# The last edge attention of a four-layer graph network: fp32 one-hots written by ScalarE from a square and a Relu

## The chip, the cores and the metric

The kernel runs on one core of a Trainium2 chip. The metric is the device time of one launch in microseconds (us). The engines are TensorE (PE, its weight loads are PEld), VectorE (DVE), ScalarE (ACT), GpSimd (POOL) and SyncE (SP, which here only issues DMAs). Each engine runs its own instructions in order, and semaphores tie them together.

## The reference, cut to what matters

Four graph layers follow one another on 3125 nodes with 256 features and 103125 edges that are sorted by destination. The change touches the edge part of the last one:

```
rel    = rel_w[edge_relations]
mod_k  = K[src] + 0.2 * rel[:, None, :]
scores = einsum('ehd,ehd->eh', Q[dst], mod_k) / D ** 0.5
seg_max = segment_max(scores, dst, num_segments=N)
ex     = exp(scores - seg_max[dst])
denom  = segment_sum(ex, dst, num_segments=N)
agg    = segment_sum((ex / denom[dst])[:, :, None] * V[src], dst, num_segments=N)
```

## The kernel before, in words

**Items and blocks.** `attention_items` is used twice: as stage `l0e` (with `first` true) for layer 0 and as stage `l3e` for the last layer. An item is 512 edges (G = 4 groups of 128, one edge per partition) that all go to one block of 128 nodes; there are NI = 228 items. Four items (BI = 4) are handled as one batch m, and there are 57 batches. Below, an item's place in its batch is called position 0, 1, 2 or 3. All loops are written out in full by Python, so each engine's order is the order of the code.

**One-hots.** Three kinds say which node an edge belongs to. `ohT` (bf16, node on the partition; L809) turns queries from nodes to edges on PE. `ohrT` (L812) does it for the 64 relations. `oh` (bf16, edge on the partition; `onehots`, L800) is written by DVE for a whole batch, 128x2048 at once, from the row of 0..127 and each edge's local node number. It is used in two places: PE's `spread` (L993) multiplies it with `flT` to hand each run's maximum to the node, and ACT's `widen` (L1045) copies it for one item at a time to fp32 as `ohf`, which PE's `sums` (L1011) multiplies with the weighted values `vw`.

**DVE, at step t** (item n = t+4): for position 1 the batch's `candidates` (L845, L847, waits for `spread`) and `block_max`; `rescale` (L888); `keys` of item n (L819: relation added to the key; waits for the gather and for PE's queries), `products` (L824), `merge` (L895), `scores` (L829); after position 2 `turned_onehots(m+2)` (L809, L812); after position 3 `onehots(m+1)` (L800); then its part of `weigh` (L879, L880) for item t-1.

**PE, at step t:** for position 0 `turn_scores` (L977); `queries(n+1)` (L963, L970); for position 0 `turn_ends` (L983, L984) and `spread` (L991 and 16 matmuls of L993); `sums(t-2)` (L1011).

**ACT, at step t** (y = t-1): for position 1 `weights` (two Exp: L1068, L1072); `widen(y)`; 4 of the 12 multiplications of `weigh(y)` (L1054); for position 0 `turned_ends` (L1062), which writes `flT` for `spread`; then the other 8 multiplications.

**POOL** gathers the keys and values: four indirect DMAs per item (L777), into a ring of SK = 10 items; the gather of item n waits until ACT and DVE have weighed item n-10.

**SP** is one queue. At the first item of each batch it issues `load_rows`: `drow` (L724), then `erow` (L728), and the latter waits for DVE's `ohrT` of the batch before:

```
if m >= 1:
    sp.wait_ge(ohrT_ready, m)
sp.dma_start(erow[:, :], ...)
```

Behind it in the same queue stand the loads of the queries `qb` (L736) and the stores of finished items (L742, for which `merge` waits four items later).

## Time and profile before

| | us |
|---|---|
| median of 3 runs | 6733.41 (6720.29 to 6738.31) |
| profiled execution | 6684.46 |
| its span, first to last instruction | 6682.8 |

| engine | busy us in the span | share |
|---|---|---|
| PE | 4332.2 | 65% |
| DVE | 3454.5 | 52% |
| ACT | 2182.9 | 33% |
| POOL | 3176.4 | 48% |

The stages follow one another and have different limits. `l3e` fills about the last quarter, from 4925 to 6545 us once it runs. A busy share over the whole span says little about it; the rows below are of this stage unless they say otherwise. In a timeline a line is: start us, duration us, engine, source line, operation, output<-input, shapes, count merged, and in brackets how long the engine had been idle before and what released it.

### The profile page before, as it was taken

How to read it: one execution, taken by the hardware profiler on the slowest of the kernel's cores; microseconds unless marked ns; L12 is line 12 of the kernel's file. 1: busy time of each engine (PE TensorE's matmuls, PEld its weight loads, DVE VectorE, ACT ScalarE, POOL GpSimd, SP SyncE). 2: the span in 40 equal slices, each digit the busy share in tenths (PEclk: the TensorE clock that was granted, in tenths of full speed). 3: DMA queues.
4: the chain of work that ended last, by engine and by line, in shares of the span. 5: the costliest groups of instructions: out<-in, count | busy, mean ns of one | idle time of the engine just before them, and what ended most of it. 6: DMA issues, size and time to landing. Idle time of an engine off the chain costs nothing. (4 is left out here: it accounts for less than half of the span.)

```text
span 6682.8 us, 90484 instructions
## 1 busy us (share of the span) xinstructions
PE 4332.2 (65%) x24913; PEld 3133.4 (47%) x24913; DVE 3454.5 (52%) x6689; ACT 2182.9 (33%) x7656; POOL 3176.4 (48%) x3187
## 2 busy tenths in 40 slices
PE   6996667777777734545444537887646666666666
PEld 4664445554444423333333436775335555555553
DVE  4453666666666661212211231112558888888885
ACT  1222455555555430000000111222224554445551
POOL 0422566666666137667766520002155565665551
PEclk8897777777777876767676778998878888888885
DMA  4334666666666525333333407872366666666673
GB/s 134 126 124 163 187 199 201 200 199 199 201 199 197 115 79 185 93 93 92 91 93 93 69 34 254 269 252 86 110 197 203 199 208 203 204 207 196 204 188 102
DMA packets 509934, 1077.05 MB, mean 161 GB/s; under 512 B 94770, under 2 KB 322388, under 8 KB 505993
## 3 DMA queue, kind: packets, MB, share of 16 engines
q0 software_dynamic: 204144, 617.42, 32.6%
q1 hardware_dynamic: 296854, 452.03, 20.2%
q10 hardware_dynamic: 8512, 2.74, 0.2%
q8 instruction: 168, 2.75, 0.2%
q14 instruction: 256, 2.10, 0.1%
HBM read 964.49 MB, written 194.54 MB: 173 GB/s over the span
## 5 line engine op out<-in xcount | busy, mean ns | idle before, releaser
L777 POOL DMA_INDIRECT l3e_kv<-t_table,k_recs x912 | 969.6, 1063 | 677.8 <-ACT l3e_vw L1054 376.5
L777 POOL DMA_INDIRECT l0e_kv<-t_table,k_recs x912 | 969.1, 1063 | 636.7 <-ACT l0e_vw L1054 374.8
L1469 PE MATMUL l2e_pA<-l2e_row,l2e_oh 128*128 128x257 f32 x1824 | 623.6, 509 | 780.2 <-issue 315.1
L1423 POOL DMA_INDIRECT l2e_row<-t_table,l2e_idx x912 | 900.7, 988 | 388.0 <-issue 268.0
L1469 PEld LDWEIGHTS l2e_pA<-l2e_row,l2e_oh 128*128 128x128 f32 x1824 | 454.0, 258 | 949.5 <-issue 862.0
L1011 PE MATMUL l0e_pA<-l0e_vw,l0e_ohf 128*128 128x260 f32 x1824 | 650.8, 492 | 199.0 <-issue 138.8
L963 PE MATMUL l3e_pQE<-l3e_qb,l3e_ohT 128*128 128x256 bf16 x2736 | 424.6, 316 | 412.1 <-issue 386.1
L1054 ACT ACTIVATE l0e_vw<-l0e_kv,l0e_w 128x64 f32<-128x64 f32 x2736 | 679.9, 334 | 0.0
L1054 ACT ACTIVATE l3e_vw<-l3e_kv,l3e_w 128x64 f32<-128x64 f32 x2736 | 679.7, 334 | 0.0
L1448 DVE SCALAR_TENSOR_TENSOR l2e_acc<-l2e_acc,k_itf,l2e_pA 128x257 f32<-128x257 f32 x228 | 109.9, 482 | 1059.8 <-issue 978.3
L1011 PEld LDWEIGHTS l0e_pA<-l0e_vw,l0e_ohf 128*128 128x128 f32 x1824 | 412.7, 239 | 366.6 <-issue 219.8
L1011 PE MATMUL l3e_pA<-l3e_vw,l3e_ohf 128*128 128x260 f32 x1824 | 532.9, 442 | 7.7 <-ACT l3e_vw L1054 7.2
L963 PEld LDWEIGHTS l3e_pQE<-l3e_qb,l3e_ohT 128*128 128x128 bf16 x2736 | 296.2, 111 | 513.5 <-issue 434.7
L963 PE MATMUL l0e_pQE<-l0e_qb,l0e_ohT 128*128 128x256 bf16 x2736 | 449.7, 326 | 72.7 <-issue 55.9
L1480 ACT ACTIVATE moe_agg<-l2e_acc 128x257 f32 x228 | 95.3, 418 | 1217.1 <-DVE l2e_acc L1448 613.5
L1011 PEld LDWEIGHTS l3e_pA<-l3e_vw,l3e_ohf 128*128 128x128 f32 x1824 | 373.7, 216 | 77.5 <-ACT l3e_vw L1054 9.8
L963 PEld LDWEIGHTS l0e_pQE<-l0e_qb,l0e_ohT 128*128 128x128 bf16 x2736 | 312.5, 116 | 190.5 <-issue 93.3
L819 DVE TENSOR_TENSOR l3e_kv<-l3e_kv,l3e_pD 128x1024 f32<-128x1024 f32 x228 | 276.0, 1211 | 171.5 <-DMA t_agg<-l0e_acc 92.5
L1971 POOL DMA_INDIRECT comb_ya<-t_yslot,k_slot x52 | 51.9, 999 | 602.8 <-POOLq L68 582.2
L1045 ACT ACTIVATE l3e_ohf<-l3e_oh 128x512 f32<-128x512 bf16 x228 | 141.0, 619 | 499.7 <-PE l3e_pA L1011 374.3
L824 DVE TENSOR_TENSOR l0e_prod<-l0e_pQE,l0e_kv 128x1024 f32<-128x1024 f32 x228 | 276.3, 1212 | 33.8 <-DMA t_table<-l0n_tab 33.3
L824 DVE TENSOR_TENSOR l3e_prod<-l3e_pQE,l3e_kv 128x1024 f32<-128x1024 f32 x228 | 279.2, 1224 | 7.8
(469 smaller groups left out, 7118.9 us busy)
## 6 DMA issues: line engine op xcount, KB each, us to landing
exp_w<-in_L_gnn_w SPq DMA_DIRECT2D x224, 512.0 KB
t_table<-l0n_tab SPq DMA_DIRECT2D x26, 2048.0 KB, 6.9
l0e_qb<-t_q SPq DMA_DIRECT2D x228, 192.0 KB
l3e_qb<-t_q SPq DMA_DIRECT2D x228, 192.0 KB
t_agg<-l0e_acc SPq DMA_DIRECT2D x228, 130.0 KB
t_agg<-l3e_acc SPq DMA_DIRECT2D x228, 130.0 KB
l0e_drow<-t_drow SPq DMA_DIRECT2D x57, 512.0 KB
l3e_drow<-t_drow SPq DMA_DIRECT2D x57, 512.0 KB
```

What stands on the lines that cost most here:

```text
L777: pool.indirect_dma_start(kv[:, n % SK, g, :], None, table[:, :], bass.IndirectOffsetOnAxis(ap=K["recs"][:, n, g, ridx:ridx + 1], axis=0)) ...
L819: dve.tensor_tensor(key, key, pR.unsqueeze(2).to_broadcast([P, G, H, DK]), ALU.add).then_inc(key_done, 1)
L824: dve.tensor_tensor(prod[:, n % 2, :, :], pQE[n % 2][:, :, :], kv[:, n % SK, :, 0:D], ALU.mult).then_inc(prod_done, 1)
L963: last = pe.matmul(pQE[n % 2][:, g, :], ohT[:, m % 2, G * j + g, :], qb[:, n % QL, i, :], start=(i == 0), stop=(i == 2))
L1011: last = pe.matmul(pA[n % 2][:, 0:H * HV], ohf[:, n % 2, g, :], vw[:, v, g, :, :].rearrange("p h c -> p (h c)"), start=(g == 0), stop=(g = ...
L1045: act.activation(ohf[:, n % 2, :, :], oh[:, m % 2, G * j:G * j + G, :], ACT.Copy).then_inc(ohf_ready, 1)
L1054: last = act.activation(vw[:, v, g, h, 0:DK], kv[:, n % SK, g, D + h * DK:D + (h + 1) * DK], ACT.Copy, scale=w[:, m % 2, j, g, h:h + 1])
L1423: pool.indirect_dma_start(row[:, s, g, 0:D], None, table[:, :], bass.IndirectOffsetOnAxis(ap=idx[:, i, g:g + 1], axis=0)).then_inc(row_rea ...
L1448: dve.scalar_tensor_tensor(out=acc[:, s, :], in0=acc[:, before, :], scalar=K["itf"][:, i, 1:2], in1=pA[s % 2][:, 0:W], op0=ALU.mult, op1=A ...
L1469: last = pe.matmul(pA[s % 2][:, 0:W], oh[:, s, g, :], row[:, s, g, :], start=(g == 0), stop=(g == G - 1))
L1480: last = act.activation(all_agg[:, bass.ds(b, 1), :].rearrange("p b c -> p (b c)"), acc[:, s, :], ACT.Copy)
L1971: pool.indirect_dma_start(ya[:, t % U, k, :], None, T["yslot"][:, :], bass.IndirectOffsetOnAxis(ap=K["slot"][:, t, k:k + 1], axis=0)).then ...
```

## The change

In the stage of the last layer (`first` false) only:

- DVE no longer writes `oh`, and that tile is gone.
- ACT makes the fp32 one-hot of an item itself, three items ahead: `near(n)` is four Square instructions of 128x128 (local node number minus 0..127, squared), and `at(n)` is one Relu of 128x512 over one minus that. It replaces `widen`.
- `ohf` has six slots instead of two.
- `spread` on PE reads `ohf` in fp32 instead of `oh` in bf16, so `flT`, `crow` and `oneb` become fp32 too. It now waits until all four items of the batch are ready.
- `run` is laid over a constant tile to save room.

```diff
+        OS = 2 if first else 6
-        oh = S.sb("oh", [P, 2, BI * G, P], BF16)
+        oh = S.sb("oh", [P, 2, BI * G, P], BF16) if first else None
+        FT = BF16 if first else F32
+        flT = S.sb("flT", [P, BI * G, 2, H], FT)
+        crow = S.sb("crow", [1, BI * G, 2, H], FT)
+        oneb = S.sb("oneb", [1, P], FT)
+        ohf = S.sb("ohf", [P, OS, G, P])
...
-                if j == 3 and m + 1 < NBT:
+                if first and j == 3 and m + 1 < NBT:
                     onehots(m + 1)
...
             def spread(m):
-                pe.wait_ge(oh_ready, m + 1)
+                if first:
+                    pe.wait_ge(oh_ready, m + 1)
+                else:
+                    pe.wait_ge(ohf_ready, BI * (m + 1))
...
+                    spot = oh[:, m % 2, c, :] if first else ohf[:, (BI * m + c // G) % OS, c % G, :]
...
+            def near(n):
+                if n >= OS:
+                    act.wait_ge(a_ps, n - OS + 1)
+                for g in range(G):
+                    last = act.activation(ohf[:, n % OS, g, :], K["iota"][:, :], ACT.Square, bias=K["dlf"][:, n, g:g + 1], scale=-1.0)
+                last.then_inc(near_done, 1)
+
+            def at(n):
+                act.wait_ge(near_done, n + 1)
+                act.activation(ohf[:, n % OS, :, :], ohf[:, n % OS, :, :], ACT.Relu, bias=K["ones"][:, 0:1], scale=-1.0).then_inc(ohf_ready, 1)
...
             for t in range(0, NI + 1):
                 m, j = divmod(t, BI)
                 y = t - 1
                 if live(m) and j == 1:
                     weights(m)
+                if not first and t + 3 < NI:
+                    near(t + 3)
                 if y >= 0:
-                    widen(y)
+                    if first:
+                        widen(y)
                     weigh(y, 0, 1)
+                if not first and t + 3 < NI:
+                    at(t + 3)
                 if live(m) and j == 0:
                     turned_ends(m)
```

## Rows read from the trace of the kernel before

**Rows 1.** Busy time per engine of the running stage (stage windows; us, busy us, count).
```profile
4925.00:6545.00 1620.00, 1092.71 (x9187) 832.53 (x9184) 1332.59 (x2314) 814.87 (x3135) 931.03 (x872) 0.82 0.67 197
```
**Rows 2.** What DVE waited for, 5100 to 6500: total us, times, longest.
```profile
DVE l3e_kv L819 <- PE l3e_pD L970: 51.0, 33, 3.4
DVE l3e_kv L819 <- DMA t_agg<-l0e_acc: 47.1, 38, 5.5
DVE l3e_cand L845 <- PE l3e_pC L993: 46.6, 40, 2.8
```
**Rows 3.** What SP's queue waited for in the same stretch.
```profile
SPq L728 <- DVE l3e_ohrT L812: 457.5, 29, 19.2
```
**Rows 4.** Timeline of one batch, from DVE's turned one-hots to the keys of position 0.
```profile
5711.34 0.74 DVE L812 TENSOR_SCALAR l3e_ohrT<-l3e_erow,k_pidx 64x2048 bf16<-64x2048 bf16 x1
5712.11 0.48 SPq L728 DMA_DIRECT2D l3e_erow<-t_erow  x1
5713.70 0.00 SPq L736 DMA_DIRECT2D l3e_qb<-t_q  x1
5716.83 2.28 DVE L800 TENSOR_TENSOR l3e_oh<-k_iotab,k_dlb 128x2048 bf16<-128x2048 bf16 x1
5717.69 2.72 PE L963 MATMUL l3e_pQE<-l3e_qb,l3e_ohT 128*128 128x256 bf16 x12 [6.89 <-issue]
5720.35 0.81 PE L970 MATMUL l3e_pD<-l3e_relw,l3e_ohrT 64*128 64x64 bf16 x12
5721.27 1.22 DVE L819 TENSOR_TENSOR l3e_kv<-l3e_kv,l3e_pD 128x1024 f32<-128x1024 f32 x1 [1.41 <-issue]
```
**Rows 5.** Timeline: keys of position 0 (first and last batch) and one held merge.
```profile
4944.67 1.22 DVE L819 TENSOR_TENSOR l3e_kv<-l3e_kv,l3e_pD 128x1024 f32<-128x1024 f32 x1 [1.79 <-PE l3e_pD L970]
5027.81 0.43 DVE L895 TENSOR_TENSOR l3e_acc<-l3e_part,l3e_pA 128x260 f32<-128x260 f32 x1 [4.95 <-DMA t_agg<-l3e_acc]
6471.09 1.22 DVE L819 TENSOR_TENSOR l3e_kv<-l3e_kv,l3e_pD 128x1024 f32<-128x1024 f32 x1 [2.45 <-PE l3e_pD L970]
```
**Rows 6.** Timeline of the same batch: from sums to candidates.
```profile
5721.09 2.02 PE L1011 MATMUL l3e_pA<-l3e_vw,l3e_ohf 128*128 128x260 f32 x8
5723.06 1.47 PE L963 MATMUL l3e_pQE<-l3e_qb,l3e_ohT 128*128 128x256 bf16 x12
5723.21 0.63 ACT L1045 ACTIVATE l3e_ohf<-l3e_oh 128x512 f32<-128x512 bf16 x1 [8.73 <-PE l3e_pA L1011]
5726.17 0.28 ACT L1062 ACTIVATE l3e_flT<-l3e_pC 128x128 bf16<-128x128 bf16 x1 [1.38 <-PE l3e_pC L984]
5726.60 0.21 PE L991 MATMUL l3e_pC<-l3e_crow,l3e_oneb 1*128 1x128 bf16 x1 [1.55 <-ACT l3e_flT L1062]
5726.74 0.56 PE L993 MATMUL l3e_pC<-l3e_flT,l3e_oh 128*128 128x8 bf16 x16
5727.33 0.22 DVE L845 COPY l3e_cand<-l3e_pC 128x64 f32<-128x64 f32 x1 [1.08 <-PE l3e_pC L993]
```
**Rows 7.** Timeline, fp32 passes that keep PE full: 64 and 128 moving columns.
```profile
3843.16 0.56 PE L1748 MATMUL gate_wide<-moe_wg,gate_xT 128*128 128x64 f32 x4
4302.74 2.05 PE L1863 MATMUL exp_pH<-exp_xT,exp_w 128*128 128x128 f32 x16
```
**Rows 8.** Timeline, the batch before: a gather released by ACT, and keys of position 2.
```profile
5700.94 0.94 POOL L777 DMA_INDIRECT l3e_kv<-t_table,k_recs  x1 [3.62 <-ACT l3e_vw L1054]
5706.83 1.22 DVE L819 TENSOR_TENSOR l3e_kv<-l3e_kv,l3e_pD 128x1024 f32<-128x1024 f32 x1 [1.02 <-DMA t_agg<-l0e_acc]
5707.97 0.95 POOL L777 DMA_INDIRECT l3e_kv<-t_table,k_recs  x1 [2.33 <-ACT l3e_vw L1054]
5708.13 2.96 ACT L1054 ACTIVATE l3e_vw<-l3e_kv,l3e_w 128x64 f32<-128x64 f32 x12
```
**Rows 9.** Groups by line: ACT with 256 and with 512 columns.
```profile
L2232 ACT ACTIVATE l3n_kv<-l3n_pK 128x512 f32<-128x512 f32 x12 | 7.1, 591 | 0.0
L2231 ACT ACTIVATE l3n_q<-l3n_pQ 128x256 bf16<-128x256 f32 x12 | 4.6, 384 | 27.3 <-PE l3n_pK L2198 27.3
```
**Rows 10.** Groups by line: the table load after the one Square of the kernel (combine stage).
```profile
L2047 ACT ACT_TABLE_LOAD x1 | 1.3, 1283 | 0.0
```

More of the change, by code:

```diff
@@ L654, in attention_items @@
         sc = S.sb("sc", [P, 2, BI * G * H])
-        run = S.sb("run", [BI * G * H, P])
+        run = S.sb("run", [BI * G * H, P]) if first else K["upper"][0:BI * G * H, :]
         fl = S.sb("fl", [BI * G * H, P], BF16)
-        flT = S.sb("flT", [P, BI * G, 2, H], BF16)
-        crow = S.sb("crow", [1, BI * G, 2, H], BF16)
-        oneb = S.sb("oneb", [1, P], BF16)
+        FT = BF16 if first else F32
+        flT = S.sb("flT", [P, BI * G, 2, H], FT)
+        crow = S.sb("crow", [1, BI * G, 2, H], FT)
+        oneb = S.sb("oneb", [1, P], FT)
         cand = S.sb("cand", [P, BI, G, H])
@@ L666, in attention_items @@
         w = S.sb("w", [P, 2, BI, G, H])
-        ohf = S.sb("ohf", [P, 2, G, P])
+        ohf = S.sb("ohf", [P, OS, G, P])
         vw = S.sb("vw", [P, VS, G, H, HV])
@@ L687, in attention_items @@
         vwa_ready, vwd_ready, a_ps, part_done, item_done = (S.sem(k) for k in ("vwa_ready", "vwd_ready", "a_ps", "part_done", "item_done"))
-        key_done, ohrT_ready = S.sem("key_done"), S.sem("ohrT_ready")
+        key_done, ohrT_ready, near_done = S.sem("key_done"), S.sem("ohrT_ready"), S.sem("near_done")
         if first:
@@ L992, in spread @@
                 for c in range(BI * G):
-                    last = pe.matmul(pM[:, c // G, c % G, :, :].rearrange("p k h -> p (k h)"), oh[:, m % 2, c, :], flT[:, c, :, :].rearrange("p k h -> p (k h)"), start=False, stop=(c == BI * G - 1))
+                    spot = oh[:, m % 2, c, :] if first else ohf[:, (BI * m + c // G) % OS, c % G, :]
+                    last = pe.matmul(pM[:, c // G, c % G, :, :].rearrange("p k h -> p (k h)"), spot, flT[:, c, :, :].rearrange("p k h -> p (k h)"), start=False, stop=(c == BI * G - 1))
                 last.then_inc(m_ps, 1)
@@ L1010, in sums @@
                 for g in range(G):
-                    last = pe.matmul(pA[n % 2][:, 0:H * HV], ohf[:, n % 2, g, :], vw[:, v, g, :, :].rearrange("p h c -> p (h c)"), start=(g == 0), stop=(g == G - 1))
+                    last = pe.matmul(pA[n % 2][:, 0:H * HV], ohf[:, n % OS, g, :], vw[:, v, g, :, :].rearrange("p h c -> p (h c)"), start=(g == 0), stop=(g == G - 1))
                 last.then_inc(a_ps, 1)
@@ L1072, in weights @@
                 act.activation(w[:, m % 2, :, :, :].rearrange("p i g h -> p (i g h)"), z[:, :], ACT.Exp).then_inc(w_ready, 1)
+            if not first:
+                for n in range(3):
+                    near(n)
+                    at(n)
             for t in range(0, NI + 1):
```

## The prediction

> **What bounds the kernel now.** I read the stage windows first, then the waits of DVE, then the timeline of one batch on all queues. In the running stage no engine is full: of 1620 us DVE is busy 1333, PE 1093, POOL 931, ACT 815 [rows 1]. So the batch of four items, which takes 1620/57 = 28.4 us, is set by a loop of waits with DVE in it, and the question is whether the instruction that goes (L800) lies on that loop.
>
> The timeline shows the loop. DVE ends the turned one-hots `ohrT` at 5712.08. SP has stood waiting for exactly that, 457.5 us in 29 waits over 1400 us [rows 3], and issues `erow` at 5712.11, and behind it in its queue the query load of position 0 at 5713.70. PE has nothing to do until that load lands, 6.89 us idle, and starts the queries at 5717.69. They take 2.72 us, and 0.81 us for the relations follow. DVE's keys of position 0 start at 5721.27, after an idle of 1.41 us [rows 4]. From the end of `ohrT` to these keys it is 9.2 us, and DVE's own work between them, L800 included, does not fill this. It is not one batch: in the timeline from 4944.67 to 6471.09, 49 of 56 batches have idle time before the keys of position 0, mean over all 1.64 us [rows 5]. The waits of keys for PE and a DMA in 1400 us are 51.0 and 47.1 us [rows 2]; they also hold position 2, below.
>
> The rest of the loop is keys of position 0, `scores`, PE's `spread`, `candidates`, items 1 and 2, and the next `ohrT`: 28.4 - 9.2 = 19.2 us. In it DVE waits for `spread` in 40 of the 49 batches of that stretch, 46.6 us [rows 2].
>
> **The change part by part.**
>
> *L800 goes from DVE.* It takes 2.28 us, 2.2 us of queue time, 57 times, 125 us of DVE's work. It lies after the scores of position 3, between `ohrT` and the keys of position 0 [rows 4]. In 49 of 56 batches the idle before these keys grows by what is removed, and nothing is gained: late next is what was late already, PE waiting for the query load. In the 7 others DVE had been held in `merge` by a store (4.95 us in the batch at 5027.81 [rows 5]) and comes late; these gain at most 2.2 us each. Per batch 2.2 x 7/56 = -0.3 us, bounds 0 and -2.2.
>
> *`spread` in fp32.* No row has an fp32 matmul with 8 moving columns. Now 16 bf16 matmuls take 0.56 us and one more 0.14 us ahead of them: 0.73 us from 5726.60 to `candidates` at 5727.33 [rows 6]. An fp32 matmul shows as two passes, each with its own weight load. The nearest row is 4 passes of 64 columns in 0.56 us, last one 0.22 us long, so one every (0.56-0.22)/3 = 0.113 us [rows 7]. Seventeen matmuls are 34 passes: 34 x 0.113 = 3.84 us, that is +3.1 us. Bounds: if 8 columns cost what the columns cost, a pass is an eighth of 0.113, and with the bf16 spacing of 0.035 us as floor (0.56/16) 34 passes take 1.2 us, +0.5; at twice the spacing 34 x 0.226 = 7.7 us, +7. I take +3.1, because weights of 128 columns are loaded in the nearest row and here alike.
>
> The same 128 columns of weights arrive at 0.035 us in bf16 [rows 6] and at 0.113 us in fp32 [rows 7]. The Trainium skill ("TensorE: Matmul & The Clock Gate", Weight-path perf modes) says why this speaks against the change: a fast weight load exists for 128 weights of any type but fp32, and a load takes columns/1.2 ns, 107 ns. By its figure the 34 passes would be an estimated 3.6 us instead of 3.84.
>
> *ACT.* `widen`, 0.63 us [rows 6], becomes four Squares and a Relu. A 64-column ACTIVATE with a scale from a tile comes every (2.96-0.33)/11 = 0.24 us [rows 8]; 64 columns more cost 64 x (591-384)/256 = 0.05 us [rows 9]. So four Squares take about 1.2 us; the Relu takes 0.6 us like `widen`, since its wait for `near` is covered by four multiplications (1 us). That is +1.2 us per item (bounds +1.0 and +1.6), 270 us of ACT's time: 815 becomes some 1090 of 1620 us, no bound by share. Queued behind it on ACT: (a) `flT` at position 0. ACT starts on the end of `sums` at 5723.21, and `flT` at 5726.17 after 1.38 us idle [rows 6]. New: 5723.21 + 1.2 + 1.0 + 0.6 + 0.1 = 5726.1, just in time. By the same sum over 52 batches the mean delay is 0.33 us (29 have none, 7 have 1.38): +0.3 us. (b) The multiplications of positions 1 to 3, one after another: they end 1.2, 2.4 and 3.6 us later plus what `candidates` is late. PE's `sums` for them come after the query wait, ACT's idle of 8.73 us [rows 6] takes this up. (c) POOL, which waits for ACT with 2.33 and 3.62 us of idle per batch [rows 8]; twelve gathers of 1.25 us fit between, with 2 us to spare.
>
> *What takes up the delay.* Keys of position 2 wait now: 1.02 us at 5706.83, 5.9 us behind the gather at 5700.94 that ACT released [rows 8], and this distance holds for 47 batches. I can't name the mechanism, but that gather follows `flT` and not `spread`, so the idle, 37 us over 56 batches, absorbs -0.7 us of the spread's +3.1. The longer `spread` also moves `sums`, `shift` and `queries` of position 2 by 3.1 us; they were 1.7 us and more ahead. The new wait of `spread` for four one-hots costs nothing: the last is written before `flT` on the same queue. The startup one-hots lie in ACT's idle time. A different table would cost 1.28 us per load [rows 10]; that load stands after the Square there, and none before it, so I put nothing.
>
> *Sum.* Per batch -0.3 + 3.1 + 0.3 - 0.7 = +2.4 to 2.5 us; times 56 = +139 us. In the profiled execution's terms 6684.5 + 139 = 6823. The runs' median lies 49 us above that execution, so the forecast for the median is 6733 + 139 = **6872 us**, and the batch grows from 28.4 to 30.9 us.
>
> **The rivals.**
> *POOL becomes late (slower still).* ACT releases the first gather after `weights` 1.2 + 3.1 us later, the loop moves by 2.5. If keys of position 0 need those gathers, each batch gets another 1 us, and where nothing is absorbed 0.7 more: 6872 + 57 to 97 = 6930 to 6970. For it: 38 keys waits lay to a DMA's account [rows 2]. Against: POOL itself still waits for ACT.
> *PE stays fast.* After 6.89 us idle the queries ran 2.72 us [rows 4] against 1.47 us at 5723.06 [rows 6]. If a late `sums` shortens that gap enough, 1.25 us and 0.3 us of the relations come back: 56 x 1.5 = 87 us, 6785.
> *Passes overlap.* With +0.5 instead of +3.1 for `spread`, all of it is absorbed at position 2 and ACT's +0.3 stays against L800's -0.3: 6733, the same.
> *DVE is the bound (faster).* Decided at the keys of position 0: if the queries land at least 2.2 us before DVE arrives, L800 is worth its full 2.2 us. That needs the query load to come 2.2 us sooner than now, for example because fewer gathers compete with it as ACT releases them late. Then -2.2 + 3.1 + 0.3 - 0.7 = +0.5, and with cheap passes -2.2 - 0.2 = -2.4 us a batch, 6733 - 134 = 6600.
> *The change doesn't do what it says*: Square sits in another table than Exp. Two loads a batch, 2 x 1.28 us on ACT, one of them ahead of `weights`: up to 57 x 2.6 = 146 us on top, 7020.
>
> **How the numbers follow.** Forecast 0.50 (its own range 6830 to 6910); PE fast or partly cheap passes, 6760 to 6830, 0.19; POOL late 0.17; the table 0.03; the same 0.05; faster 0.06. Within 0.3% (20 us) is about what a measurement can tell from no change. Range 6765 to 6965. Faster 0.06, same 0.06, slower 0.88.
>
> **What would show it.** L993 with twice as many records, one every 0.11 us and `candidates` idle before it grown from 1.2 to above 3 us; idle before keys of position 0 near 3.5 us; keys of position 2 hardly idle; POOL still waiting for ACT; PE still 2.72 us in the first queries. I am wrong if the fp32 passes come every 0.05 us or less, if the idle before the keys of position 0 does not grow, or if SP no longer waits for `ohrT`.

## The result, and the profile after

The kernel after takes **7303.18 us** (median of 4 runs, 7299.61 to 7306.93) against 6730.88 (4 runs, 6720.29 to 6738.31): ratio **1.0852**, 95% interval 1.0833 to 1.0870. The forecast was 6872 with a range to 6965. The direction was right, the size was not: +139 us were expected and +572 came, 10.2 us a batch in place of 2.5.

The stage window of the running stage, after (columns as in [rows 1]):

```profile
6000.00:6700.00 700.00, 498.57 (x3256) 405.13 (x3257) 384.39 (x715) 343.91 (x1265) 281.64 (x286) 0.72 0.50 150
```

Against [rows 1] DVE is 55% busy and not 82%, the DMA engines 0.50 and not 0.67, and PE's mean granted clock is 0.72 and not 0.82. Everything got emptier but PE, which is 71% busy and not 67%: a loop of waits has become longer, and PE does its part of it at a lower clock. What DVE, ACT and POOL waited for, 5200 to 6900 (total us, times, longest), answers [rows 2]. DVE waits in two places, ahead of the keys of position 0 and ahead of the candidates:

```profile
DVE l3e_kv L821 <- DMA t_agg<-l0e_acc: 392.7, 39, 10.8
DVE l3e_cand L847 <- PE l3e_pC L999: 299.1, 42, 10.4
```
```profile
ACT l3e_ohf L1057 <- DMA t_table<-l12n_hs: 341.9, 39, 9.1
```
```profile
POOL l3e_kv L779 <- ACT l3e_vw L1071: 820.0, 88, 10.7
```

There are two new waits on DVE: the candidates wait 7.1 us a time for `spread` (299.1/42; before 46.6/40 = 1.2 in [rows 2]), and the keys of position 0 wait 10.1 us a time (392.7/39). The name of a DMA beside the keys is not to be trusted: `t_agg<-l0e_acc` is a transfer of another stage. ACT's Squares (L1057) carry an equally foreign name, and all they wait for in the code is PE's `sums`.

PE's timeline through one `spread` answers [rows 6]:

```profile
5898.94 0.76 PE L996 MATMUL l3e_pC<-l3e_crow,l3e_oneb 1*128 1x128 f32 x2 [0.46 <-ACT l3e_flT L1079]
5899.63 7.00 PE L999 MATMUL l3e_pC<-l3e_flT,l3e_ohf 128*128 128x8 f32 x32
5906.48 3.81 PE L1017 MATMUL l3e_pA<-l3e_vw,l3e_ohf 128*128 128x260 f32 x8
```

The 32 passes take 7.00 us and start every 0.213 us, against 0.113 in [rows 7]. The `sums` behind them take 3.81 us. The same eight passes behind the bf16 `spread` of the kernel before take less:

```profile
5727.15 3.14 PE L1011 MATMUL l3e_pA<-l3e_vw,l3e_ohf 128*128 128x260 f32 x8
```

The stage windows of that stretch after the change (last three columns: granted clock, DMA share, GB/s) say why:

```profile
5898.00:5900.00 2.00, 1.34 (x6) 0.99 (x6) 1.68 (x4) 1.48 (x7) 0.00 (x0) 0.50 0.30 81
5902.00:5904.00 2.00, 2.00 (x11) 2.00 (x11) 0.00 (x0) 0.00 (x0) 1.48 (x2) 0.50 0.83 309
```

PE idles ahead of `spread`, the granted clock has fallen to 0.50 (1.2 GHz) when it begins, and it stays there through 7 us in which PE is busy all the time. So it is in 54 of the 57 batches of this trace.

The batch's other half answers [rows 4]: from DVE's turned one-hots to the keys of position 0, first DVE and PE, then SP and ACT, then POOL's last gather of twelve.

```profile
5917.35 0.74 DVE L814 TENSOR_SCALAR l3e_ohrT<-l3e_erow,k_pidx 64x2048 bf16<-64x2048 bf16 x1
5934.35 1.22 DVE L821 TENSOR_TENSOR l3e_kv<-l3e_kv,l3e_pD 128x1024 f32<-128x1024 f32 x1 [10.69 <-DMA t_agg<-l0e_acc]
```
```profile
5923.57 2.72 PE L965 MATMUL l3e_pQE<-l3e_qb,l3e_ohT 128*128 128x256 bf16 x12 [5.41 <-issue]
5926.23 0.82 PE L972 MATMUL l3e_pD<-l3e_relw,l3e_ohrT 64*128 64x64 bf16 x12
5926.97 2.32 PE L1017 MATMUL l3e_pA<-l3e_vw,l3e_ohf 128*128 128x260 f32 x8
```
```profile
5922.02 0.34 SPq L738 DMA_DIRECT2D l3e_qb<-t_q  x1
5924.15 0.01 SPq L744 DMA_DIRECT2D t_agg<-l3e_acc  x1
5927.73 0.02 SPq L738 DMA_DIRECT2D l3e_qb<-t_q  x1
5932.74 0.71 SPq L744 DMA_DIRECT2D t_agg<-l3e_acc  x1
5934.30 0.34 SPq L738 DMA_DIRECT2D l3e_qb<-t_q  x1
```
```profile
5934.37 1.28 ACT L1057 ACTIVATE l3e_ohf<-k_iota,k_dlf 128x128 f32<-128x128 f32 x4 [9.00 <-DMA t_table<-l12n_hs]
```
```profile
5916.35 1.20 POOL L779 DMA_INDIRECT l3e_kv<-t_table,k_recs  x1 [10.70 <-ACT l3e_vw L1071]
...
5931.22 0.95 POOL L779 DMA_INDIRECT l3e_kv<-t_table,k_recs  x1 [0.30 <-issue]
```

From the end of `ohrT` (5918.09) to the end of PE's relation terms (5927.05) it is 9.0 us, as before: PE was late in the same way. But the keys start only at 5934.35, **7.3 us behind** what they need from PE, and ACT's Squares at 5934.37, 5.1 us behind the end of the `sums` they need (5929.29). Both start again right behind POOL's twelfth gather in a row (ends 5932.17). I call this the late release. Over 56 batches the median distance from PE's relation terms to the keys of position 0 is 6.5 us after and 0.15 us before.

PE's ends are modelled, but the order of PE's work says more. The keys wait for the relation terms and the Squares for the `sums` that run 2.3 us longer on the same engine, and yet both start within 0.02 us of each other, in nine of ten batches. The trace's records of the semaphores agree: the signal of the relation terms is recorded at 5934.26 and that of the `sums` at 5934.35. Had the matmuls themselves run late, the two would lie some 2 us apart, as they do in a trace of this program without the late release, below (1.95 us or more). So the signal of the relation terms was held back when their work was done. Nor is it PE's signals alone. The last semaphore that SP asks for between 5924.15 and 5934.16 was set at 5916.21. But its register instructions, which stand between two DMA issues, come mostly every 0.7 us there, and the issues lie 3.6 and 5.0 us apart. From item 10 to item 218, 367 of 1872 such steps of SP are longer than 0.6 us (325 us in all), and 98 in the kernel before.

### The profile page after: what moved, and what is told of

Same layout as the page of the kernel before. It is cut to its first block and busy times, and to the rows that moved or that the text cites. A ratio compares the mean times of both kernels' runs of the same rounds, so it can differ in the third digit from the quotient of the medians.

```text
span 7299.5 us, 92996 instructions
## 1 busy us (share of the span) xinstructions
PE 4781.4 (66%) x25882; PEld 3576.6 (49%) x25882; DVE 3324.5 (46%) x6632; ACT 2469.2 (34%) x8568; POOL 3090.2 (42%) x3187
## 5 line engine op out<-in xcount | busy, mean ns | idle before, releaser
L779 POOL DMA_INDIRECT l3e_kv<-t_table,k_recs x912 | 902.4, 989 | 1310.1 <-ACT l3e_vw L1071 1053.6
L1071 ACT ACTIVATE l3e_vw<-l3e_kv,l3e_w 128x64 f32<-128x64 f32 x2736 | 695.5, 334 | 0.0
L1017 PE MATMUL l3e_pA<-l3e_vw,l3e_ohf 128*128 128x260 f32 x1824 | 578.3, 471 | 9.8 <-ACT l3e_vw L1071 9.7
L1017 PEld LDWEIGHTS l0e_pA<-l0e_vw,l0e_ohf 128*128 128x128 f32 x1824 | 429.6, 247 | 248.6 <-issue 133.5
L965 PEld LDWEIGHTS l3e_pQE<-l3e_qb,l3e_ohT 128*128 128x128 bf16 x2736 | 299.1, 112 | 443.9 <-issue 362.2
L1017 PEld LDWEIGHTS l3e_pA<-l3e_vw,l3e_ohf 128*128 128x128 f32 x1824 | 405.5, 234 | 89.5 <-ACT l3e_vw L1071 12.5
L1057 ACT ACTIVATE l3e_ohf<-k_iota,k_dlf 128x128 f32<-128x128 f32 x912 | 288.8, 387 | 467.8 <-DMA t_table<-l12n_hs 440.5
L999 PEld LDWEIGHTS l3e_pC<-l3e_flT,l3e_ohf 128*128 128x128 f32 x1824 | 392.3, 331 | 12.5 <-issue 12.1
L999 PE MATMUL l3e_pC<-l3e_flT,l3e_ohf 128*128 128x8 f32 x1824 | 397.7, 361 | 0.0
```

What stands on the lines that cost most here:

```text
L779: pool.indirect_dma_start(kv[:, n % SK, g, :], None, table[:, :], bass.IndirectOffsetOnAxis(ap=K["recs"][:, n, g, ridx:ridx + 1], axis=0)) ...
L965: last = pe.matmul(pQE[n % 2][:, g, :], ohT[:, m % 2, G * j + g, :], qb[:, n % QL, i, :], start=(i == 0), stop=(i == 2))
L999: last = pe.matmul(pM[:, c // G, c % G, :, :].rearrange("p k h -> p (k h)"), spot, flT[:, c, :, :].rearrange("p k h -> p (k h)"), start=Fa ...
L1017: last = pe.matmul(pA[n % 2][:, 0:H * HV], ohf[:, n % OS, g, :], vw[:, v, g, :, :].rearrange("p h c -> p (h c)"), start=(g == 0), stop=(g ...
L1057: last = act.activation(ohf[:, n % OS, g, :], K["iota"][:, :], ACT.Square, bias=K["dlf"][:, n, g:g + 1], scale=-1.0)
L1071: last = act.activation(vw[:, v, g, h, 0:DK], kv[:, n % SK, g, D + h * DK:D + (h + 1) * DK], ACT.Copy, scale=w[:, m % 2, j, g, h:h + 1])
```

## The experiments

Two questions stood at the start: does the fp32 `spread` cost its full length, and does the keys' wait come out of it, or out of ACT's work and POOL's gathers? (The letters A and B in the expectations are theory and rival, as each text works them out.) In each diff lines without a sign are context. All times are beside runs of the kernel before in the same set, whose median is given, because the sets differ by 10%: the kernel before takes 6685 to 6741 us in the first, the second and the fifth ("the slower sets", and the result above was like them), and 6057 us in the third and the fourth ("the faster sets"). The expectations call this a difference of chips. The record doesn't bear that out: it gives the sets the chip numbers 4, 15, 13, 15 and 10, and number 15 has both a slower set (6740.63) and a faster one (6057.48). What makes a set slow is not known.

**First set (before: 6684.79 us).** *17 narrow fp32 matmuls*, whose result nothing reads, ahead of the bf16 `spread`:

```diff
                 pe.wait_ge(flT_ready, m + 1)
+                if not first:
+                    for c in range(17):
+                        pe.matmul(pC[:, 384:392], K["ident"][:, :], K["iota"][:, 0:8], start=True, stop=True)
```

> The kernel before, with 17 fp32 matmuls of 8 moving columns (identity as weights, into unused PSUM columns) in front of the bf16 spread of the last edge attention; ACT and DVE as before. The output is that of before. Theory A (the whole loss is the fp32 spread, and what follows from it): the passes come every 0.22 us, as in the changed kernel, so 34 of them are 7.4 us; candidates wait about 8 us instead of 1.2, and the gathers that ACT releases after candidates start later too, so the keys of position 0 wait as well and the time comes near the changed kernel's: 7200 to 7300 us. Rival B (the fp32 spread is a plain delay, the wait of the keys of position 0 comes from ACT's Squares): +7.4 - 0.7 us a batch, 57 x 6.7 = 380: about 7110, with the idle before the keys of position 0 under 3 us. Rival C (my prediction's price, passes every 0.11 us): 6850 to 6900.

Measured: 7075.64 us, ratio 1.0582 (1.0551 to 1.0613), +391 us or 7.0 a batch. PE's timeline of one batch:

```profile
5727.98 6.51 PE L993 MATMUL l3e_pC<-k_iota,k_ident 128*128 128x8 f32 x34 [1.58 <-ACT l3e_flT L1065]
...
5735.09 3.81 PE L1014 MATMUL l3e_pA<-l3e_vw,l3e_ohf 128*128 128x260 f32 x8
```

The 34 passes alone take 6.7 us in the median (4.3 to 7.4) and the batch pays all of it, in the wait of the candidates (334.1 us in 37 waits from 5100 to 6500). The keys' waits stay near what they were, 41.5 us for PE and 11.0 under a DMA's name, so nothing couples `spread` to them. That is about rival B's size.

*ACT makes the one-hots that `sums` needs*, DVE still writes `oh`, `spread` stays bf16:

```diff
                 if y >= 0:
-                    widen(y)
+                    if first:
+                        widen(y)
+                    else:
+                        near(y)
                     weigh(y, 0, 1)
+                    if not first:
+                        at(y)
```

> The kernel before, with only widen in the last edge attention replaced by four Squares and a Relu for the same item (no lead, two slots); DVE still writes the bf16 one-hots and spread stays bf16. Theory A: ACT's extra 1.2 us per item is nearly hidden, 6730 to 6800 us, candidates still wait 1 to 1.6 us. Rival B: ACT's later release of the gathers is what costs, then this kernel alone shows keys of position 0 waiting 5 us and more and takes 7000 us or more.

Measured: 6833.10 us, 1.0219 (1.0190 to 1.0249), +148 us or 2.6 a batch; the keys wait 123.8 us in 35 waits of the kind with a foreign DMA name. That lies between what the two texts expected. So ACT's work isn't hidden in this set, and 2.6 + 7.0 = 9.6 of the 10.2 us are found in the two parts.

*No gathers past the first ring of ten items:*

```diff
-            for n in range(NI):
+            for n in range(NI if first else SK):
...
-                dve.wait_ge(kv_ready[n % SK], 16 * G * (n // SK + 1))
+                dve.wait_ge(kv_ready[n % SK], 16 * G * (n // SK + 1) if first else 16 * G)
```

The later items compute on stale keys and values.

> The changed kernel; in the last edge attention only the first ring of ten items is gathered and the later items compute on those stale keys and values (part of the work left out, outputs are wrong). Theory A (the keys of position 0 wait until the run of twelve gathers is through): their idle of about 9.3 us goes, the candidates still wait 7 us, and the batch falls from 39.3 to some 31 to 33 us: 6830 to 6950 us. Rival D (the wait belongs to PE or to SP's query loads, not to the gathers): the batch stays above 38 us and the time above 7250.

Measured: 6825.22 us, 1.0208 (1.0178 to 1.0237). The candidates still wait for `spread`, the keys' waits are PE's again (94.9 us in 44 waits), the foreign-named ones are gone: the keys of position 0 start 0.11 us (median) behind PE's relation terms. Of SP's 1872 steps 5 are over 0.6 us. What holds the keys needs POOL's gathers. `spread` is shorter here too, 5.6 us from its start to the candidates (median) where after has 7.7.

*ACT writes bf16 one-hots three items ahead and widens them*; DVE writes none, `spread` is bf16:

```diff
-        FT = BF16 if first else F32
+        FT = BF16
...
-                act.activation(ohf[:, n % OS, :, :], ohf[:, n % OS, :, :], ACT.Relu, ...
+                act.activation(ohb[:, n % OS, :, :], sqf[:, :, :], ACT.Relu, ...
...
-                    if first:
-                        widen(y)
+                    widen(y)
```

> A version of the change that keeps spread in bf16: ACT squares into one fp32 slot, Relu writes a bf16 one-hot three items ahead, and widen copies it to fp32 as before; DVE writes none. ACT does 1.8 us more per item than before. Theory A: with the fp32 spread gone most of the loss is gone, 6720 to 6850 us, candidates wait 1 to 2 us. Rival B (ACT's load is what costs): 7000 us or more, as ACT does more here than in the changed kernel. If DVE's L800 had been on the path, the time would fall to 6650 or below.

Measured: 6950.76 us, 1.0395 (1.0358 to 1.0433). What DVE waited for, 5100 to 6500:

```profile
DVE l3e_kv L823 <- DMA t_agg<-l0e_acc: 418.8, 46, 10.7
...
DVE l3e_cand L849 <- PE l3e_pC L1001: 0.4, 2, 0.2
```

With bf16 the wait for `spread` is gone and the keys' wait is there in full, 9.1 us a time. The two waits have two causes. The time lies between what theory and rival expected: a loss of 4.8 us a batch is left without the fp32 `spread`.

**Second set (before: 6740.63 us): what is it in the gathers?** *Half the bytes*, number and order of the gathers unchanged (the second half of each row stays stale, and half rows are read by whole-row indices, so the results are others):

```diff
-                    pool.indirect_dma_start(kv[:, n % SK, g, :], None, table[:, :],
+                    wid, rows = (2 * D, table[:, :]) if first or n < SK else (D, table.rearrange("n (t d) -> (n t) d", t=2))
+                    pool.indirect_dma_start(kv[:, n % SK, g, 0:wid], None, rows,
```

> The kernel after, but in the last stage each gather past the first ring of ten items fetches half a row (256 floats for each edge, through a view of the table with rows half as long, by the same indices), so that its bytes are halved and the number, the order and the release of the gathers stay. It computes other scores and stale values. In dispute is why the keys of position 0 stand idle 9.3 us after the change. Theory bytes: twelve gathers that ACT releases late and together bring 12 x 256 KB = 3.1 MB in one run, the DMA engines are full for 17 us, and what the other engines need stands behind it. Halved, the run's bytes pass while POOL still issues: the keys' idle time ahead falls from 393 us in all to under 100, and the kernel takes 6830 to 6900. Theory run: twelve gathers that POOL issues without a pause hold the releases up, whatever they bring: idle time stays at 350 to 400, and the time within 1% of 7260.

Measured: 7304.25 us, 1.0847 (1.0815 to 1.0878), the same as after. What DVE waited for, 5100 to 6500, and a window inside one such wait:

```profile
DVE l3e_kv L822 <- DMA t_agg<-l0e_acc: 349.0, 36, 10.8
```
```profile
5853.00:5855.00 2.00, 0.27 (x1) 0.00 (x0) 0.00 (x0) 0.00 (x0) 1.38 (x2) 1.00 0.35 117
```

The wait is as long while the DMA engines are 0.35 busy at 117 GB/s. The bytes are ruled out. Whether it is POOL's issuing or the number of rows (128 for each gather in both kernels) this run can't tell.

*A pause behind each item's gathers:*

```diff
+                if not first:
+                    for _ in range(4):
+                        pool.memset(scr[:, :], 0.0)
+                        pool.drain()
```

> The kernel after, with four memsets of 64 columns, each followed by a drain, on POOL behind the four gathers of each item (nothing is left out of the computation). It puts a pause of some 1 to 2 us into POOL's run, and spreads the gathers' transfers a little. Theory run: the releases pass in the pause; the keys of position 0 no longer idle 9 us, and the kernel falls towards 6900 to 7000. Theory bytes: the transfers still come together; the idle time stays within 20% of 393 us, and the time near 7250 to 7350.

Measured: 7355.63 us, 1.0923 (1.0891 to 1.0955). POOL's timeline:

```profile
5856.09 0.18 POOL L784 MEMSET l3e_scr<- 128x64 f32 x1
5860.05 0.69 POOL L784 MEMSET l3e_scr<- 128x64 f32 x3 [3.78 <-issue]
```

The pause was not the 1 to 2 us that I wanted: from the first memset to the second it is 3.4 us in the median (2.9 to 5.1 in nine of ten). With ten us an item POOL became the bound itself (370.5 us of keys waits, now honestly for `l3e_kv<-t_table`). The run doesn't tell the theories apart by its time. But SP's steps over 0.6 us have fallen from 367 to 69, which fits that it takes gathers without a pause.

*POOL released one item later*, nothing else:

```diff
-                    pool.wait_ge(vwa_ready, n - SK + 1)
-                    pool.wait_ge(vwd_ready, n - SK + 1)
+                    pool.wait_ge(vwa_ready, n - hold + 1)
+                    pool.wait_ge(vwd_ready, n - hold + 1)
```

Here `hold` is SK - 1.

> The kernel before, but in the last stage POOL waits for one item more (the weighing of item n-9, not n-10) ahead of each item's gathers, which is what a ring of nine items would do. Nothing is added to ACT, to PE or to DVE. Theory: that POOL's gathers come some 5 us later is enough to make the idle time ahead of keys, and explains most of the +148 us that ACT's own one-hots cost the kernel before; expected +80 to +200. Rival: ACT's longer chain itself costs this (its factor and weights come later), and the later gathers alone give within 0.5% of the kernel before.

Measured: 6726.26 us, 0.9987 (0.9973 to 1.0002). My theory fell: in the kernel before, gathers that come later cost nothing by themselves.

*17 wide fp32 matmuls*, 128 columns for 8:

```diff
+                        pe.matmul(pC[:, 384:512], K["ident"][:, :], K["iota"][:, 0:128], start=True, stop=True)
```

> The kernel before with 17 fp32 matmuls of 128 moving columns, not 8, ahead of each spread of the last stage (34 passes; their result is not read). Theory: the fall of the granted clock to 0.5 comes from narrow passes, which leave PE's array idle between weight loads. At 128 columns it stays at 1.0 and a pass takes 0.12 to 0.13 us (half of the 0.25 us of a pass of 260 columns): 4.3 us a batch, +245 us at most, under the +391 us of the narrow ones though it does 16 times the work. Rival: any block of fp32 passes this long falls to 0.5; then the passes take 0.25 us each, 8.5 us a batch, and +450 to +500.

Measured: 7047.01 us, 1.0465 (1.0434 to 1.0495), +306 us or 5.5 a batch, between theory and rival. Sixteen times the columns cost less than the narrow ones. PE's timeline and the windows of one batch:

```profile
5741.31 5.37 PE L993 MATMUL l3e_pC<-k_iota,k_ident 128*128 128x128 f32 x34 [2.32 <-ACT l3e_flT L1065]
...
5747.19 2.00 PE L1014 MATMUL l3e_pA<-l3e_vw,l3e_ohf 128*128 128x260 f32 x8
```
```profile
5742.00:5744.00 2.00, 2.00 (x11) 2.00 (x10) 0.00 (x0) 1.07 (x5) 0.66 (x1) 0.50 0.12 47
5744.00:5746.00 2.00, 2.00 (x19) 2.00 (x19) 0.00 (x0) 0.00 (x0) 1.39 (x3) 0.97 0.42 119
```

and the windows of the narrow ones:

```profile
5726.00:5728.00 2.00, 0.24 (x3) 0.16 (x3) 1.65 (x4) 0.44 (x3) 1.70 (x2) 1.00 0.77 209
5728.00:5730.00 2.00, 2.00 (x14) 2.00 (x14) 0.00 (x0) 1.74 (x8) 0.08 (x1) 0.74 0.93 348
5732.00:5734.00 2.00, 2.00 (x11) 2.00 (x11) 0.00 (x0) 0.00 (x0) 1.39 (x3) 0.50 0.69 207
```

The price of a pass is the same for both widths: one starts every 0.112 us while the granted clock is 1.00 and every 0.213 us at 0.50. What differs is the clock. The wide passes shown start at 0.50 and it rises to 1.00 under them; the narrow ones start at 1.00 and it falls to 0.50 under them. This holds over all 57 blocks of each trace. At the end of the narrow passes the clock is low in 57 (12 start low, in 45 it falls during them, in none it rises), at the end of the wide ones it is high in 57 (17 are never low, in 40 it rises during them). The `sums` behind take 3.81 and 2.00 us. That it falls at all isn't put on the narrow passes by this: PE had been idle 2.2 us ahead of the block (median of both kernels), and under the wide passes it falls too, in 17 blocks. The medians of the blocks, 6.7 us narrow and 5.7 us wide (4.0 to 7.0), lie closer together than the two batches that are shown.

**Third and fourth set: the chain, and the comparison that was removed.** In the third set the kernel before takes 6056.6 us, and the kernel after wasn't in it. So the fourth set has it beside three of the same kernels, with before at 6057.48; only the fourth is used for after and the two that break POOL's run.

*The comparison of 128 x 2048 back in its place*, into a free buffer:

```diff
-                if first and j == 3 and m + 1 < NBT:
-                    onehots(m + 1)
+                if j == 3 and m + 1 < NBT:
+                    onehots(m + 1) if first else spare(m + 1, n)
```

> The kernel after, with one comparison more on DVE at the place where the kernel before wrote its one-hots (the same operation over 128 x 2048 values, into a buffer of the products that is free then; nothing reads it). Does taking that operation away bring anything? Theory gap: the operation lies in the middle of POOL's run of gathers and lengthens one of them; without it twelve gathers run in one piece, and PE's releases pass only after the last. With it back the keys' idle time ahead falls from 393 us to under 150, and the kernel is FASTER than after by 150 to 350 us (ratio to before 1.035 to 1.06), though it does more. Rival: it is only work; it stands in the wait ahead of the keys of position 0 and costs nothing (ratio 1.083 to 1.087).

> The kernel after with the comparison of 128 x 2048 back on DVE in its old place. Theory gap: it breaks POOL's run, and the keys wait under half of what they do in after_same; ratio 0.02 to 0.04 under that one. Rival, only work: ratio within 0.003 of after_same, with the keys' wait shorter by the 2.2 us of the comparison, which stands in it.

*One memset behind each item's gathers*, no drain:

```diff
+                if not first:
+                    if n:
+                        pool.wait_ge(scr_done, n)
+                    pool.memset(scr[:, :], 0.0).then_inc(scr_done, 1)
```

> The kernel after, with one memset of 64 columns (0.17 us) on POOL behind the four gathers of each item, and no drain. The memset keeps POOL's queue of gathers in step without the 3.0 to 4.6 us that each drain took in the kernel with the gap. Theory: an operation of another kind between gathers lets the releases pass, as the drains did for ACT (its squares of position 3 followed PE's sums by 0.8 us there); the keys' idle time falls under 200 us and the kernel to a ratio of 1.04 to 1.06. Rival: the memset is queued like the gathers and changes nothing: ratio 1.083 to 1.09.

> The kernel after with one memset of 64 columns on POOL behind each item's gathers. Theory: it breaks the run for the late release, ratio 0.02 to 0.04 under after_same. Rival: it changes nothing, ratio within 0.003 of after_same.

*The load of the queries ahead of the row loads*, in the kernel after and in the kernel before:

```diff
+                    if not first:
+                        load_queries(n)
                     if n % BI == 0 and n // BI + 1 < NBT:
                         load_rows(n // BI + 1)
-                    load_queries(n)
+                    if first:
+                        load_queries(n)
```

> The kernel after, with SP's load of the queries of position 0 issued ahead of that batch's row loads, and no longer behind the wait for the turned relation one-hots. PE's queries of position 0 can start some 4 us sooner, ahead of most of POOL's run. Theory loop: from the turned one-hots over SP, the load, PE's queries and the keys is what bounds the batch; keys of position 0 then lose some 4 us of their 9.3 us of waiting, ratio near 1.05. Rival, releases held by POOL's run: PE is early but the keys still start 2 us after the last gather; ratio 1.08 to 1.087.

> The kernel after with the load of the queries of position 0 ahead of the row loads, on the same chip as after_same. Theory: the chain over SP's load accounts for all of the keys' wait, since POOL's run, started by the weighing that follows on the same keys, is only in the way when PE's queries fall into its end. The wait goes (under 0.5 us a batch) and the ratio is 0.03 to 0.06 under that of after_same. Rival: on a chip with the late release, the keys still start some 2 us after POOL's last gather: wait over 5 us, ratio within 0.015 of after_same.

> The kernel before with the same reordering on SP. Nothing is left out. The keys of position 0 wait 1.6 us a batch there, PE's queries of position 0 wait 6.9 us for their load. If that chain is what the keys wait for, up to 1.6 us x 56 = 90 us go (ratio 0.987 to 0.995). Rival: the gathers' release sets the wait, and the ratio is 0.998 to 1.002.

*The kernel after itself:*

> The kernel after, unchanged, to stand beside the three below on one chip. On a chip where the kernel before takes 6680 to 6740 us: ratio 1.085, keys of position 0 idle 9.3 us, starting 7 us behind PE's relation terms. On one where it takes some 6060 us: if the late release is a matter of the chip, the keys start 0.1 us behind PE's relation terms and wait some 3.5 us, ratio 1.055 to 1.062, as the kernel with the memset did; if it is a matter of POOL's unbroken run, they wait 9 us there too, and the ratio is over 1.09.

| kernel | us | ratio to before (95%) |
|---|---|---|
| after | 6414.94 | 1.0588 (1.0557 to 1.0619) |
| after, comparison back | 6429.63 (third set 6432.15) | 1.0612 (1.0581 to 1.0643) |
| after, memset | 6407.02 (6414.37) | 1.0575 (1.0544 to 1.0606) |
| after, queries first | 6201.04 (6199.03) | 1.0235 (1.0205 to 1.0265) |
| before, queries first (third set) | 5946.50 | 0.9819 (0.9801 to 0.9837) |

In this set the same program costs +357 us and not +572. What DVE waited for in after here, 5000 to 6200, and the keys of position 0 in one batch (DVE, PE and ACT, then the gathers beside it):

```profile
DVE l3e_kv L821 <- PE l3e_pD L972: 127.6, 50, 5.0
```
```profile
5286.96 1.22 DVE L821 TENSOR_TENSOR l3e_kv<-l3e_kv,l3e_pD 128x1024 f32<-128x1024 f32 x1 [3.61 <-PE l3e_pD L972]
```
```profile
5286.26 0.59 PE L972 MATMUL l3e_pD<-l3e_relw,l3e_ohrT 64*128 64x64 bf16 x12
5286.78 2.02 PE L1017 MATMUL l3e_pA<-l3e_vw,l3e_ohf 128*128 128x260 f32 x8
```
```profile
5288.84 1.28 ACT L1057 ACTIVATE l3e_ohf<-k_iota,k_dlf 128x128 f32<-128x128 f32 x4 [3.72 <-PE l3e_pA L1017]
```
```profile
5286.97 0.95 POOL L779 DMA_INDIRECT l3e_kv<-t_table,k_recs  x1 [0.30 <-issue]
```

The keys start 0.11 us behind PE's relation terms, in the middle of POOL's run, and ACT's Squares 1.9 us later, behind the `sums`. There is no late release here; the wait is 3.5 us (median), it is the chain over SP's load, and the name beside it is the right one. Of SP's 1872 steps 5 are over 0.6 us. Putting the comparison back costs 14.7 us, less than these runs can tell from nothing, and the keys' wait is 1.9 us shorter: the theory of the gap has nothing to explain in this set, and the rival (only work) is borne out. With the queries first the keys wait for nothing, and 214 us come back.

`spread` is not as dear here as in the first sets. One batch:

```profile
5292.37 6.20 PE L999 MATMUL l3e_pC<-l3e_flT,l3e_ohf 128*128 128x8 f32 x32
```
```profile
5292.00:5294.00 2.00, 2.00 (x14) 1.88 (x14) 0.00 (x0) 1.75 (x8) 0.00 (x0) 0.82 0.91 307
5294.00:5296.00 2.00, 2.00 (x11) 2.00 (x10) 0.00 (x0) 0.00 (x0) 1.68 (x2) 0.50 0.72 221
```

The passes start at full clock in 56 of 57 batches and it falls under them; they take 5.6 us in the median and not 7.0, and from the start of `spread` to the candidates it is 6.1 us and not 7.7.

The two traces of the one program also show where a slower set loses its time: only where POOL gathers. The stages without gathers are equally long (`l0n` 610 and 610 us, `gate` 143 and 143, `exp` 591 and 591, `fin` 125 and 125, by the first and last record of their tiles), the three with gathers are not (`l0e` 1656 and 1324, `l2e` 1315 and 1180, `l3e` 2275 and 1862), and these three make 880 of the 881 us between the two spans. `l0e` and `l2e` are not touched by the change.

**Fifth set (before: 6688.47 us): the same reordering in a set with the late release.**

> The kernel after with the load of the queries of position 0 ahead of the row loads, once more, for a chip on which the kernel before takes 6680 to 6740 us. There after stands at 1.085, with the keys idle 9.3 us. Theory: PE's relation terms are done 6 us sooner, before POOL's run is long, so that the late release has nothing to hold: wait under 1 us, ratio 1.01 to 1.03. Rival: the release comes late whenever POOL's run is unbroken; wait over 4 us, ratio 1.05 to 1.08. On the other kind of chip (before near 6060 us) it repeats 1.023.

> The kernel before with the same load ahead. On a chip with before at 6680 to 6740 us: theory, up to the 1.6 us a batch that its keys of position 0 wait, ratio 0.98 to 0.99; rival, the wait moves to the late release elsewhere (keys of position 2, the candidates), ratio over 0.995. On the other kind of chip it repeats 0.982.

Measured: after with the queries first 7147.35 us, 1.0682 (1.0648 to 1.0716); before with the queries first 6783.37 us, **1.0138** (1.0109 to 1.0168), slower, where in the third set it was 0.9819. What DVE waited for in the former, 5000 to 6600:

```profile
DVE l3e_cand L850 <- PE l3e_pC L1002: 508.4, 44, 14.3
DVE l3e_kv L824 <- DMA t_agg<-l0e_acc: 100.5, 11, 9.9
```

The keys are mostly free, as the theory said, but the candidates now wait 11.6 us a time, 4.5 us more than in after. They follow `spread` at once; what comes late is ACT's `flT` ahead of it, more than 1 us behind PE's transposes in 43 of 57 batches (5 in after). In the latter, one batch (PE, DVE, POOL):

```profile
5383.57 0.59 PE L996 MATMUL l3e_pC<-l3e_flT,l3e_oh 128*128 128x8 bf16 x16
```
```profile
5391.55 0.23 DVE L848 COPY l3e_cand<-l3e_pC 128x64 f32<-128x64 f32 x1 [8.43 <-DMA moe_bg<-in_L_gnn_bg]
```
```profile
5389.15 0.94 POOL L780 DMA_INDIRECT l3e_kv<-t_table,k_recs  x1 [0.30 <-issue]
```

`spread` is over at 5384.16 by its record, and the candidates, which wait for nothing else, start at 5391.55, 1.5 us behind the end of POOL's last gather. The same line of the same program in the third set:

```profile
4640.36 0.56 PE L996 MATMUL l3e_pC<-l3e_flT,l3e_oh 128*128 128x8 bf16 x16
```
```profile
4640.95 0.23 DVE L848 COPY l3e_cand<-l3e_pC 128x64 f32<-128x64 f32 x1
```
```profile
4640.40 1.03 POOL L780 DMA_INDIRECT l3e_kv<-t_table,k_recs  x1 [0.30 <-issue]
```

0.03 us, beside a running gather. So the late release isn't tied to the keys or to ACT's one-hots: in the slower sets a release by PE that falls into POOL's run shows up late, and the reordering only chose another victim. "Wait under 1 us, ratio 1.01 to 1.03" was wrong.

## Why the prediction went wrong, by its own steps

**The term that was mis-sized: `spread` in fp32, +3.1 us.** I took 0.113 us for a pass from [rows 7] and kept 7.7 us (0.226 each) as the upper bound. Measured from the start of `spread` to the candidates are 7.7 us (median) against 0.73 before: +7.0, at the bound. The spacing was right at full clock (0.112 us). What failed is that it was taken for the spacing here. PE waits ahead of these passes, they start at a granted clock of 0.50 in 54 of 57 batches, and it does not rise under them: 0.213 us each. The row for it was there: [rows 4] has queries of 2.72 us where [rows 6] has 1.47, PE at half clock after a wait. I used that pair for a rival in which PE becomes faster, and not for the price of `spread`. My range didn't hold my own bound either: with +7 in place of +3.1 the sum gives some 7090 us, and the range ended at 6965. By the figure of the Trainium skill ("TensorE: Matmul & The Clock Gate", LDWEIGHTS (loading the stationary operand)), quoted in the prediction, the passes would take an estimated 3.6 us. The traces agree with its 107 ns at a granted clock of 1.00 (0.112 us) and not at 0.50 (0.213 us).

**The term that was put at nothing: "twelve gathers of 1.25 us fit between, with 2 us to spare", and ACT's "hidden" +1.2 us an item.** ACT's terms were right in size (four Squares 1.26 us, Relu 0.70), POOL did have time and did wait for ACT (820.0 us). But in the first set ACT's one-hots alone cost 2.6 us a batch. With the +7.0 this makes 9.6 of the 10.2 us. My rival "POOL becomes late" gave 1 to 1.7 us a batch and a wrong mechanism: no transfer was late. Half the bytes change nothing, a later release of POOL's gathers changes nothing in the kernel before, no gathers at all remove the wait. In before the distance was visible ("5.9 us behind the gather ... I can't name the mechanism"): the keys of position 2 start 1.7 us (median of 47) behind PE's relation terms there. In the faster sets it is 0.11 us, in after and in before with the queries first. I priced it as something that absorbs 0.7 us. That the wait grows with POOL's unbroken run, from nine gathers to twelve ahead of the keys of position 0 (medians of before and after), fits the traces but was not tested.

**In the faster set the sum doesn't close either.** There +357.5/56 = 6.4 us a batch were measured. Putting +7.0 for +3.1 into my sum gives 6.35, but that agreement is luck: in this set `spread` costs +5.3 (6.1 us against 0.73), and the -0.7 has nothing to absorb, since the keys of position 2 wait 0.1 us a batch in before with the queries first. So -0.3 + 5.3 + 0.3 = 5.3, and 1.1 us a batch stays unexplained. No trace of the kernel before exists from a faster set, so the parts can't be read side by side. What came as forecast there is the idle time "near 3.5 us" ahead of the keys of position 0 (median 3.5), and the price of L800: -0.3 us a batch was forecast, and putting it back costs 14.7/56 = 0.26, which is about the runs' resolution and consistent with it.

**Point by point, of what would show it.** Twice the records in `spread`: yes; every 0.11 us: no, 0.21. Candidates idle above 3 us: yes, 7.1. Keys of position 0 near 3.5: in the faster set yes, in the slower one 9.1 in the mean. Keys of position 2 hardly idle: yes, 8.5 us in all 56 batches. POOL waiting for ACT: yes. PE's first queries at 2.72 us: yes. SP still waiting for `ohrT`: yes, erow is issued at 5918.11, 0.02 us behind it. No table load was added.

**What stays open.** Why signals come late, and SP's register instructions slowly, beside POOL's gathers in some sets and not in others. What is shown: it takes gathers, not their bytes; it holds back PE's signals to DVE and to ACT, and SP's own steps, at the same time; it ends 1.6 to 2.6 us behind the end of POOL's last gather in after; and it is absent in the sets with before at 6057 us, in the same program. It isn't shown that it belongs to a chip. A break of POOL's run by one memset or by DVE's comparison was tried only in the faster set, which doesn't need it, and with drains in a slower one, where POOL became the bound. The 3.8 us a batch between the sets (10.2 - 6.4) are a difference of two ratios; `spread` has 1.7 of them (7.0 - 5.3).

No version here beats the kernel before in both kinds of set. Before with the queries first is 1.8% faster in one and 1.4% slower in the other.

## What to carry to other kernels

- When PE waits ahead of a stage, price the stage at both levels of the clock, with rows at either. Here a block of 32 narrow fp32 passes took 5.6 to 7.0 us (medians) where the spacing at full clock gives 3.6, and the work behind it paid as well. Turning a bf16 operand to fp32 to save a copy on another engine was the dearest part of this change.
- An instruction that stands inside a wait brings next to nothing when it is removed, whatever its length (2.28 us removed here, 0.26 us gained).
- When a wait carries a name that can't be its cause, look at what starts at the same instant on the other engines. Two engines that wait for two different results of one engine and start together say that signals were held, not work.
- Repeat a surprising loss in another set of runs before explaining it, since a reordering that gains in one can lose in the other, and a sum that closes should be checked term by term in the set it is held against.

## What the runs showed of the hardware that I had not expected

- fp32 passes with 128 weight columns start every 0.112 us at a granted clock of 1.00 and every 0.213 us at 0.50, whether 8 or 128 columns move.
- Behind the same idle time of PE (2.2 us in the median) the granted clock was low at the end of each of 57 blocks of 34 passes of 8 columns, and high at the end of each of 57 blocks of 34 passes of 128 columns. The narrow blocks took 6.7 us in the median, the wide ones 5.7.
- The same program takes 6057 us in some sets of runs and 6685 to 6741 in others, and the stages without gathers don't differ. In the latter, starts that depend on PE lie up to 8.5 us behind PE's record beside a run of gathers (the candidates of before with the queries first); in the former mostly 0.03 to 0.11 us.
- A gather's record on POOL is 0.95 us, but a memset and a drain behind four of them take 3.4 us in the median (POOL's timeline of the kernel with the pause).
- Beside DVE's comparison for `ohrT` (5917.35) POOL's gather is longer, 1.80 us at 5917.86 where its neighbours take 0.95 (the kernel after). The Trainium skill ("DMA: Bandwidth & Descriptors", SWDGE vs HWDGE vs iDMA) says that DVE locks GpSimd out of SBUF in its 2-port mode, and that GpSimd writes descriptors there. The traces don't contradict it, but the gather outlasts the comparison by 1.6 us, so no run here shows that this is the cause.
